# Two graph layers over a dense adjacency matrix: finished block columns taken ahead of their rows, and whole-block transfers

## The chip, the cores and the metric

The kernel runs on one core of a Trainium2 chip. The metric is the device time of one execution in microseconds (us), from the start to the end of the program; lower is better. Three runs of the kernel before took 955.02, 955.76 and 956.75 us (median 955.76). One further execution was profiled; it took 956.43 us, and all rows shown are its rows.

## The reference

With x of 8192 nodes by 64 features and a dense float32 matrix adj of 8192 by 8192, two residual layers are computed:

```
h = relu(layernorm(x));  x = x + adj @ (h * keep / 0.9)      # layer 1, keep = (u >= 0.1)
h = relu(layernorm(x));  x = x + adj @ (h @ W) + b           # layer 2
```

Layer 2 of any node needs the whole of layer 1 for all nodes whose features it sums, so adj (268 MB) is needed twice, and it does not fit on the chip.

## The kernel before

adj is cut into 16 by 16 blocks of 512 by 512 (1 MB each). Block (i, k) joins the 512 nodes of row i to the features of column k. For layer 1, row i needs the blocks (i, 0) to (i, 15). When row i is complete, its new x and then its layer-2 features h2 are computed, and only then may any block of *column* i be used for layer 2. The host lays a block out so that a partition finds its part in one contiguous run; with `PARTS = 2` a block is moved as two half blocks (512 KB each, 4 KB per partition), each into one of `SLOTS = 33` slots of `blocks`.

Work is a list of items (`order_of_items`, L75). A *step* is one 128-row tile of a block multiplied for two 64-row halves of the array at once. Kinds of item:

- `one`: a block for layer 1 alone, even and odd tiles on the two halves (2 steps);
- `both`: block (s, j) below the diagonal, with column j already finished, for layer 1 of row s on one half and layer 2 of row s on the other (4 steps);
- `pair`: two blocks (2p, k) and (2p+1, k) above the diagonal for layer 2, one on each half (4 steps); their layer 1 was done earlier;
- `mix`: layer 2 of a diagonal block beside layer 1 of another block (4 steps).

A block above or on the diagonal has to be on the chip twice, first as `one`, later as `pair` or `mix`. Where it lies near the diagonal (`stays`, L48, with `KEPT = 3`) it is held in its slots in between; the others are read from memory again. Row after row, `order_of_items` takes the items of row s, mixes in the layer-2 items of column s-1 (`late`) at least 10 us after the row began (`ROW_LEAD`, in `merged`, L52), so that h2 of row s-1 is ready, and adds as many of the rereading `pair` items (`again`) as the estimated balance of transfers and matmuls allows; what is left follows after the last row.

`plan` (L111) turns the items into loads, slots and PSUM banks. A slot is taken again by the load that comes next in order, and SP, which issues all loads in order (L275 to L281), first waits until the item that last used the slot is done (`part_used`). `row_sums` has one bank for each parity of the row; `banks` has four for the layer-2 sums (`Sum`); the sums of a `pair` or `mix` item are closed at once, those of the `both` items of a row at the row's end, and VectorE adds each closed sum to `acc` in SBUF (`add_sum`, L412, L419). TensorE waits for `sum_added` before it reuses a bank.

At the end of row s ScalarE copies the row's sums to SBUF (L342), TensorE runs one more item and then transposes them with 8 small matmuls (`turn_row`, L504, L513), and VectorE makes x and h2 of the row (`row_of_layer_1`, L388 to L410), with one square root on ScalarE (L344) and the addition of the bias b (L403). After the last items of each pair of rows, `turn_pair` (L517) multiplies `acc` by W and turns it, VectorE adds it to `rows` (L429, L431), and SP stores.

At the start, SP issues x and u in nine groups (18 transfers, L273 and L274) ahead of the blocks. Per group VectorE, ScalarE and POOL make the layer-1 features (`centre_x` to `drop_x`, L308, L313, L378); POOL's queue also loads W twice and b, spread to all partitions (L300 to L302), and clears `acc` last (L316).

Of the kernel before, what the change touches and what calls it, by code (L numbers as in the profile page):

```python
# [4 lines left out]
P = 128  # L5
N = 8192
# [4 lines left out]
PARTS = 2  # L11
# [14 lines left out]
class Item:  # L26

# [13 lines left out]
class Sum:  # L41


    def __init__(self, p, half, n):
        self.p, self.half, self.first = p, half, n
# [28 lines left out]

def order_of_items():  # L75
    items, waiting = [], []
    for s in range(BLOCKS + 1):
        ones, both, late = [], [], []
        k = s - 1
        if s < BLOCKS:  # L80
            far = [j for j in range(s, BLOCKS) if not stays(s, j)]
            near = [j for j in range(s, BLOCKS) if stays(s, j)]
            ones = [Item("one", [(s, j)], j, s) for j in (near + far if s == 0 else far + near[::-1])]
            both = [Item("both", [(s, j)], j, s) for j in range(s - 1)]
        if s:
            if k % 2 == 0:
                other = ones.pop(0)
                late.append(Item("mix", [(k, k), other.blocks[0]], k, s))
            for p in range(PAIRS - 1, -1, -1):
                if 2 * p + 1 <= k:  # L90
                    t = Item("pair", [(2 * p, k), (2 * p + 1, k)], k)
                    if stays(2 * p, k):
                        late.append(t)
                    else:
                        waiting.append((s + (s < BLOCKS), t))
        again = [t for at, t in waiting if at <= s]
        if s < BLOCKS:
            spare = 2 * STEP * (BLOCKS + s) + 4 * STEP * len(late)
            again = again[:max(0, int((0.97 * spare - BLOCKS * BLOCK_LOAD) / (2 * BLOCK_LOAD - 4 * STEP * 0.97)))]
        waiting = [w for w in waiting if w[1] not in again]  # L100
        if s == BLOCKS:
            items += [t for t in again if t.k < k] + late + [t for t in again if t.k == k]
        else:
            if s:
                late.append(Item("both", [(s, k)], k, s))
            items += merged([both, ones, again, late], ROW_LEAD)
    assert not waiting
    return items


def plan():  # L111
# [42 lines left out]
    for n, t in enumerate(items):  # L154
        if t.kind == "pair":
            t.sum = Sum(t.blocks[0][0] // 2, None, n)
            sums.append(t.sum)
        elif t.kind == "mix":
            t.sum = Sum(t.k // 2, 0, n)
            sums.append(t.sum)  # L160
        elif t.kind == "both":
            if t.row not in row_sum:
                row_sum[t.row] = Sum(t.row // 2, t.row % 2, n)
                sums.append(row_sum[t.row])
            t.sum = row_sum[t.row]
        if t.sum is not None:
            t.sum.last = n
    for index, q in enumerate(sorted(sums, key=lambda q: q.last)):
        q.index = index
# [12 lines left out]
    return items, loads, sums, row_first, row_last, row_end, pair_end, finals  # L182


def bass_gnn(nc, x, adj, u, w, b, out):
# [3 lines left out]
    items, loads, sums, row_first, row_last, row_end, pair_end, finals = plan()  # L189
    closing = {q.last: q for q in sums}  # L190
    final_of = {p: n for n, p in enumerate(finals)}
    final_end = {pair_end[p]: p for p in finals}
    END = len(items)

    with ExitStack() as ctx:  # L195
# [11 lines left out]
        acc = sb("acc", [P, PAIRS, BLK])  # L207
        sums_sb = sb("sums_sb", [P, 2, BLK])
# [24 lines left out]
        x_arrived = [sem(f"x_arrived{n}") for n in range(len(GROUPS))]  # L233
        u_arrived = [sem(f"u_arrived{n}") for n in range(len(GROUPS))]
        weights_arrived = sem("weights_arrived")
        cleared = sem("cleared")
# [13 lines left out]
        row_copied = sem("row_copied")  # L250
        turned_ready = sem("turned_ready")
# [17 lines left out]
        @block.sync  # L269
        def _(sp):  # L270
            for g in range(len(GROUPS)):
                t = group_tiles(g)
                sp.dma_start(rows[:, t, :], x[:, t, :]).then_inc(x_arrived[g], 16)  # L273
                sp.dma_start(u_sb[:, t, :], u[:, t, :]).then_inc(u_arrived[g], 16)  # L274
            for load in loads:  # L275
                before = load["before"]
                if before is not None:
                    sp.wait_ge(part_used, PARTS * before["until"] + before["part"] + 1)
                i, k = load["block"]
                sp.dma_start(blocks[:, load["slot"], :], adj[(i * BLOCKS + k) * PARTS + load["part"], :, :])\  # L280
                    .then_inc(block_arrived[load["slot"]], 16)  # L281
            for n, p in enumerate(finals):
                t = slice(2 * p * TILES, (2 * p + 2) * TILES)
                sp.wait_ge(rows_ready, n + 1)
                sp.wait_ge(turned_taken, BLOCKS + n + 1)
                sp.dma_start(out[:, t, :], rows[:, t, :]).then_inc(stored, 16)
            sp.wait_ge(stored, 16 * PAIRS)

        @block.gpsimd
        def _(pool):  # L290
# [11 lines left out]
            pool.dma_start(bias[:, :], b.rearrange("(a n) -> a n", a=1).to_broadcast([P, D]))\  # L302
                .then_inc(weights_arrived, 16)

            for g, (k0, k1) in enumerate(GROUPS):
                t = group_tiles(g)
                pool.wait_ge(u_arrived[g], 16)
                nc.gpsimd.tensor_scalar(u_sb[:, t, :], u_sb[:, t, :], DROP, 1.0 / (1.0 - DROP),  # L308
                                        ALU.is_ge, ALU.mult).then_inc(keep_ready, 1)
                pool.wait_ge(keep_ready, g + 1)  # L310
                pool.wait_ge(x_scale, g + 1)
                shape = [P, (k1 - k0) * TILES, D]
                nc.gpsimd.tensor_tensor(u_sb[:, t, :], u_sb[:, t, :], square[:, t].unsqueeze(2).to_broadcast(shape),  # L313
                                        ALU.mult).then_inc(keep_scaled, 1)
            pool.wait_ge(xd_ready, len(GROUPS))
            nc.gpsimd.memset(acc[:, :, :], 0.0).then_inc(acc_cleared, 1)  # L316

        @block.scalar
        def _(act):
# [18 lines left out]
            for s in range(BLOCKS):  # L338
                act.wait_ge(part_used, PARTS * (max(row_last[s]) + 1))
                if s >= 2:  # L340
                    act.wait_ge(turned_ready, s - 1)
                nc.scalar.activation(sums_sb[:, s % 2, :], row_sums[:, s % 2, :], ACT.Copy).then_inc(row_copied, 1)  # L342
                act.wait_ge(h2_summed, s + 1)
                nc.scalar.activation(dev2[:, :], square2[:, :], ACT.Sqrt, bias=eps[:, 0:1], scale=1.0 / D)\  # L344
                    .then_inc(h2_dev, 1)

        @block.vector
        def _(dve):
# [7 lines left out]
            def centre_x(g):  # L356
                t = group_tiles(g)
                shape = [P, t.stop - t.start, D]
                dve.wait_ge(x_arrived[g], 16)
# [28 lines left out]
            def row_of_layer_1(s):  # L388
# [23 lines left out]
            def add_sum(q):  # L412
                at = slice(0, P) if q.half is None else slice(q.half * D, (q.half + 1) * D)
                dve.wait_ge(part_used, PARTS * (q.last + 1))
                if q.index == 0:
                    dve.wait_ge(acc_cleared, 1)
                else:
                    dve.wait_ge(sum_added, q.index)
                nc.vector.tensor_tensor(acc[at, q.p, :], acc[at, q.p, :], banks[at, q.bank, :], ALU.add)\  # L419
                    .then_inc(sum_added, 1)  # L420

            def pair_of_rows(p):
# [4 lines left out]
                if n == 0:  # L427
                    dve.wait_ge(biased, BLOCKS)
# [14 lines left out]

            for n in range(END + 2):
                if n in closing:
                    add_sum(closing[n])
                if n - 1 in row_end:
                    row_of_layer_1(row_end[n - 1])
                if n - 1 in final_end:
                    pair_of_rows(final_end[n - 1])  # L450

        @block.tensor
        def _(pe):
# [16 lines left out]

            def layer_2(t, parts, j, half):
# [6 lines left out]
            def multiply(t):  # L478
                s = t.row
                if s is not None and t.n == min(row_first[s]) and s >= 2:  # L480
                    pe.wait_ge(row_copied, s - 1)
                if s == 0:
                    pe.wait_ge(xd_ready, GROUP_OF[t.k] + 1)
                if t.sum is not None:
                    pe.wait_ge(h2_ready, t.k + 1)
                    if t.n == t.sum.first and t.sum.before is not None:
                        pe.wait_ge(sum_added, t.sum.before.index + 1)
# [16 lines left out]
            def turn_row(s):  # L504
# [4 lines left out]
                pe.wait_ge(row_copied, s + 1)  # L509
                for j in range(TILES):  # L510
# [6 lines left out]
            def turn_pair(p):  # L517
                n = final_of[p]
                if n == 0:
                    pe.wait_ge(weights_arrived, 48)  # L520
                pe.wait_ge(turned_taken, BLOCKS + n - 1)
                pe.wait_ge(sum_added, closing[pair_end[p]].index + 1)
# [38 lines left out]
```

## Time and profile before

| | |
|---|---|
| runs | 955.02, 955.76, 956.75 us |
| profiled execution | 956.43 us, of which the span from first to last instruction is 954.6 us |
| TensorE matmuls busy | 914.5 us (96%), 4480 records |
| VectorE, ScalarE, GpSimd busy | 141.7 us, 23.7 us, 33.7 us |
| DMA | 351.00 MB, 95.6% of 16 engines on the block queue |
| blocks moved | 656 half blocks, 344 MB |

A float32 matmul leaves two records in this profile, so a step (two matmuls) is four records. The busy time of TensorE counts a half of the array that works while the other half waits, and the modelled ends of matmuls run into the waits that follow; the time by which the work of TensorE is late has to be taken from the start times. The chain of work that ended last, in order of time, and the tables by stretch show where it waits.

### The profile page before, as it was taken

To read this page: it belongs to the slowest core of one execution; us is meant where nothing else is said; L and a number is where in the kernel's file an instruction comes from. 1 tells how busy PE (TensorE), PEld (TensorE's weight loads), DVE (VectorE), ACT (ScalarE), POOL (GpSimd) and SP (SyncE) were. 2 spreads that over 40 slices of the span, in tenths; PEclk is the share of its full clock that TensorE was granted. 3 is DMA by queue.
4 is the path that set the end of the run, shared out by engine and by line. 5 is a ranking of instruction groups with operands and counts; after the bars stand their busy time and mean duration, and the time that the engine had idled before them with its cause. 6 is when DMAs were issued, how large, how long until landed. Compare 5 with 4: busy or idle time off the path is not lost.

```text
span 954.6 us, 10490 instructions
## 1 busy us (share of the span) xinstructions
PE 914.5 (96%) x4480; PEld 348.6 (37%) x4480; DVE 141.7 (15%) x301; ACT 23.7 (2%) x52; POOL 33.7 (4%) x31
## 2 busy tenths in 40 slices
PE   2888899999999999999999999999999999999998
PEld 0112232333444444443344423443434444443444
DVE  6310101101010101010010100100100200200223
ACT  2100000000000000000000000000000000000000
POOL 7600000000000000000000000000000000000000
PEclk9999999999999999999999999999999999999999
DMA  9999999999999899989999899899899999999992
GB/s 326 410 409 409 409 410 409 409 410 388 410 380 396 297 408 368 381 289 395 361 328 367 291 328 382 333 365 390 315 355 410 364 381 403 368 366 409 409 394 76
DMA packets 98349, 351.00 MB, mean 368 GB/s; under 512 B 10960, under 2 KB 11504, under 8 KB 98304
## 3 DMA queue, kind: packets, MB, share of 16 engines
q1 hardware_dynamic: 98208, 350.27, 95.6%
q8 instruction: 36, 0.59, 0.3%
q0 software_dynamic: 96, 0.07, 0.1%
q14 instruction: 9, 0.07, 0.0%
HBM read 348.19 MB, written 2.10 MB: 367 GB/s over the span
## 4 chain that ended last, share of the span: by engine, by line
PE 83%; DMA 13%; SPq 4%; issue 0%; DVE 0%; DVEq 0%
PE banks L473 45%; PE row_sums L467 37%; DMA blocks<-in_adj 13%; SPq L280 3%; PE turned L526 1%; PE turned L513 1%; SPq L273 0%; SPq L274 0%; DVE rows L429 0%; DVEq L195 0%
## 5 line engine op out<-in xcount | busy, mean ns | idle before, releaser
L467 PE MATMUL row_sums<-blocks,features 128*64 128x512 f32 x2048 | 689.6, 598 | 34.1 <-DMA blocks<-in_adj 31.9
L473 PE MATMUL banks<-blocks,features 128*64 128x512 f32 x2048 | 673.5, 592 | 2.8 <-DMA blocks<-in_adj 2.8
L467 PEld LDWEIGHTS row_sums<-blocks,features 128*64 128x64 f32 x2048 | 213.2, 137 | 327.9 <-issue 238.9
L473 PEld LDWEIGHTS banks<-blocks,features 128*64 128x64 f32 x2048 | 224.9, 137 | 262.4 <-issue 259.6
L419 DVE TENSOR_TENSOR acc<-acc,banks 128x512 f32<-128x512 f32 (+1 forms) x87 | 59.7, 686 | 713.5 <-PE banks L473 640.0
L342 ACT ACTIVATE sums_sb<-row_sums 128x512 f32<-128x512 f32 x16 | 9.6, 597 | 777.7 <-PE banks L473 431.7
L308 POOL TENSOR_SCALAR acc<-acc 128x512 f32<-128x512 f32 (+1 forms) x9 | 18.8, 2092 | 0.8
L393 DVE TENSOR_TENSOR rows<-rows,turned 128x256 f32<-128x256 f32 x16 | 6.7, 421 | 79.8 <-PE turned L513 79.8
L513 PEld LDWEIGHTS turned<-fold,sums_sb 128*64 128x64 f32 x256 | 10.8, 138 | 8.5 <-issue 8.5
L513 PE MATMUL turned<-fold,sums_sb 128*64 128x64 f32 x256 | 10.5, 222 | 0.0
L526 PEld LDWEIGHTS turned<-pair_w,acc 128*64 128x64 f32 x128 | 7.9, 137 | 3.8 <-issue 3.8
L313 POOL TENSOR_TENSOR acc<-acc,square 128x512 f32<-128x512 f32 (+1 forms) x9 | 8.5, 946 | 3.6 <-DVE square L373 3.1
L526 PE MATMUL turned<-pair_w,acc 128*64 128x128 f32 x128 | 8.6, 273 | 0.0
L397 DVE TENSOR_TENSOR centred<-rows,total 128x256 f32<-128x256 f32 x16 | 6.8, 425 | 0.5
L399 DVE TENSOR_TENSOR squares<-centred 128x256 f32<-128x256 f32 x16 | 6.8, 425 | 0.6
L407 DVE SCALAR_TENSOR_TENSOR features<-centred,square 128x256 f32<-128x256 f32 x16 | 6.8, 425 | 0.6
L400 DVE TENSOR_REDUCE square<-squares 128x4 f32<-128x256 f32 x16 | 6.7, 420 | 0.5
L395 DVE TENSOR_REDUCE total<-rows 128x4 f32<-128x256 f32 x16 | 6.7, 420 | 0.5
L344 ACT ACTIVATE dev<-square,eps 128x4 f32<-128x4 f32 x16 | 4.8, 297 | 81.5 <-DVE square L400 81.5
L403 DVE TENSOR_TENSOR rows<-rows,bias 128x256 f32<-128x256 f32 x16 | 6.6, 415 | 0.0
L368 DVE TENSOR_REDUCE square<-features 128x8 f32<-128x512 f32 (+1 forms) x9 | 5.6, 627 | 5.0 <-ACT features L323 5.0
L378 DVE SCALAR_TENSOR_TENSOR features<-features,acc 128x512 f32<-128x512 f32 (+1 forms) x9 | 5.8, 643 | 3.0 <-POOL acc L313 2.8
(25 smaller groups left out, 43.1 us busy)
## 6 DMA issues: line engine op xcount, KB each, us to landing
blocks<-in_adj SPq DMA_DIRECT2D x656, 512.0 KB, 7.8
out<-rows SPq DMA_DIRECT2D x8, 256.0 KB, 2.0
rows<-in_x SPq DMA_DIRECT2D x7, 256.0 KB, 6.8
acc<-in_u SPq DMA_DIRECT2D x7, 256.0 KB, 6.7
rows<-in_x SPq DMA_DIRECT2D x2, 128.0 KB, 2.2
acc<-in_u SPq DMA_DIRECT2D x2, 128.0 KB, 2.5
pair_w<-in_w POOLq DMA_DIRECT2D x2, 16.0 KB, 3.7
bias<-in_b POOLq DMA_DIRECT2D x1, 32.0 KB, 5.5
```

What stands on the lines that cost most here:

```text
L280: sp.dma_start(blocks[:, load["slot"], :], adj[(i * BLOCKS + k) * PARTS + load["part"], :, :])\
L308: nc.gpsimd.tensor_scalar(u_sb[:, t, :], u_sb[:, t, :], DROP, 1.0 / (1.0 - DROP), ALU.is_ge, ALU.mult).then_inc(keep_ready, 1)
L313: nc.gpsimd.tensor_tensor(u_sb[:, t, :], u_sb[:, t, :], square[:, t].unsqueeze(2).to_broadcast(shape), ALU.mult).then_inc(keep_scaled, 1)
L342: nc.scalar.activation(sums_sb[:, s % 2, :], row_sums[:, s % 2, :], ACT.Copy).then_inc(row_copied, 1)
L397: link2(nc.vector.tensor_tensor(centred2[:, :, :], mine, total2[:, :].unsqueeze(2).to_broadcast(shape), ALU.add))
L399: link2(nc.vector.tensor_tensor(squares2[:, :, :], centred2[:, :, :], centred2[:, :, :], ALU.mult))
L407: nc.vector.scalar_tensor_tensor(out=features[:, tiles_of(s), D:2 * D], in0=centred2[:, :, :], scalar=0.0, in1=square2[:, :].unsqueeze(2). ...
L419: nc.vector.tensor_tensor(acc[at, q.p, :], acc[at, q.p, :], banks[at, q.bank, :], ALU.add)\
L467: return nc.tensor.matmul(row_sums[at, s % 2, :], features[:, k * TILES + j, 0:D], tile_of(parts, j), start=first and t.n == row_first[s][ ...
L473: return nc.tensor.matmul(banks[at, t.sum.bank, :], features[:, t.k * TILES + j, D:2 * D], tile_of(parts, j), start=t.n == t.sum.first and ...
L513: done = nc.tensor.matmul(turned[at, s % 2, j * D:(j + 1) * D], sums_sb[:, s % 2, nodes:nodes + D], fold[:, :], start=True, stop=True)
L526: done = nc.tensor.matmul(turned[at, n % 2, j * P:(j + 1) * P], acc[:, p, nodes:nodes + D], pair_w[:, :], start=True, stop=True)
```

## The change

1. `PARTS = 1`, `SLOTS = 15`: a block moves as one transfer of 1 MB (8 KB per partition) into one of 15 whole slots, and its slot is free when its whole item is done. In bytes, 15 whole slots stand where 16.5 stood.
2. `KEPT = 2` instead of 3: fewer blocks are held on the chip between their two uses.
3. `first_rows` orders rows 0 to 3 by a small clock of its own (array and transfer). In it, as soon as h2 of row s-1 is thought to be ready (`H2_LEAD`), column s-1 is taken downwards: beside the items of the rows in progress come items `ahead`, block (i, s-1) for i up to 9, for s = 1, 2, 3, that is 8 + 7 + 6 = 21 blocks. Each is used for layer 1 and layer 2 at once, as `both` is, long before row i is at hand. Its two sums go to the two halves of one of the four `banks`; VectorE adds the layer-2 half to `acc` and the layer-1 half to a new buffer `ahead` in SBUF. At the end of each of the rows 2 to 9 ScalarE copies only one half of `row_sums`, and VectorE adds `ahead` to the other half (`join_ahead`), on which `turn_row` now waits as well (`row_joined`).
4. x and u come in two halves each: 4 transfers of 1 MB instead of 18.
5. b is loaded by POOL's queue after row 7, and added in one instruction for rows 0 to 8 in row 8, then row by row. `ahead` is cleared on POOL after `acc`; the first sum waits for both.
6. The estimate for the `again` items uses 2.49 us per block, and counts the items that are really left in a row.

The diff, cut to its core:

```diff
--- before.py
+++ after.py
...
-PARTS = 2
+PARTS = 1
...
-KEPT = 3
-SLOTS = 33
+KEPT = 2
+SLOTS = 15
+
+AHEAD_ROWS, AHEAD_TO = 3, 10
 SUM_BANKS = 4
 
-STEP, BLOCK_LOAD, ROW_LEAD = 0.858, 2.545, 10.0
+
...
+HALF = N // P // 2
+HALF_OF = [k0 * TILES // HALF for k0, _ in GROUPS]
...
+BIAS_ROW = 8
...
+def layer_2_of(k, ones, waiting):
+    late = []
+    if k % 2 == 0:
+        other = ones.pop(0)
+        late.append(Item("mix", [(k, k), other.blocks[0]], k, k + 1))
+    for p in range(PAIRS - 1, -1, -1):
+        if 2 * p + 1 <= k:
+            t = Item("pair", [(2 * p, k), (2 * p + 1, k)], k)
+            if stays(2 * p, k):
+                late.append(t)
+            else:
+                waiting.append((min(k + 2, BLOCKS), t))
+    if k + 1 < BLOCKS:
+        late.append(Item("both", [(k + 1, k)], k, k + 1))
+    return late
+def layer_1_of(s):
+    far = [j for j in range(s, BLOCKS) if not stays(s, j)]
+    near = [j for j in range(s, BLOCKS) if stays(s, j)]
+    return [Item("one", [(s, j)], j, s) for j in (near + far if s == 0 else far + near[::-1])]
+def first_rows(waiting):
+    items, kept, taken, ready = [], [], set(), []
+    more, here = [], set()
+    array = transfer = 0.0
+    def put(t):
+        nonlocal array, transfer
+        for b in t.blocks:
+            if b in here:
+                here.discard(b)
+            else:
+                transfer += BLOCK_LOAD
+                array = max(array, transfer + LANDING)
+                if t.kind != "pair" and b[1] >= b[0] and stays(*b):
+                    here.add(b)
+        array += t.steps * STEP
+        items.append(t)
+    for s in range(AHEAD_ROWS + 1):
+        ones = layer_1_of(s)
+        own = [Item("both", [(s, j)], j, s) for j in range(s - 1) if (s, j) not in taken]
+        if s:
+            for t in layer_2_of(s - 1, ones, waiting):
+                (kept if all(b in here for b in t.blocks) else more).append(t)
+            more += [Item("ahead", [(i, s - 1)], s - 1, i) for i in range(s + 1, AHEAD_TO)]
+        own += ones
+        while own or any(t.row == s for t in kept + more):
+            kept_now = [t for t in kept if ready[t.k] <= array]
+            more_now = [t for t in more if ready[t.k] <= array]
+            if kept_now and (array < transfer + BLOCK_LOAD + LANDING or not (own or more_now)):
+                t = kept_now[0]
+            elif more_now:
+                t = more_now[0]
+            elif own:
+                t = own[0]
+            else:
+                array = min(ready[t.k] for t in kept + more)
+                continue
+            for queue in (kept, more, own):
+                if t in queue:
+                    queue.remove(t)
+            if t.kind == "ahead":
+                taken.add(t.blocks[0])
+            put(t)
+        ready.append(array + H2_LEAD)
+    return items, kept + [t for t in more if t.kind != "ahead"], taken
 def order_of_items():
+    waiting = []
+    items, left, taken = first_rows(waiting)
+    for s in range(AHEAD_ROWS + 1, BLOCKS + 1):
+        ones = layer_1_of(s)
+        both = left + [Item("both", [(s, j)], j, s) for j in range(s - 1) if s < BLOCKS and (s, j) not in taken]
...
+        if s == BLOCKS:
+            items += [t for t in again if t.k < s - 1] + late + [t for t in again if t.k == s - 1]
+        else:
+            work = STEP * sum(t.steps for t in ones + both + late)
+            loads = BLOCK_LOAD * (len(ones) + len(both) + 1)
+            again = again[:max(0, int((0.97 * work - loads) / (2 * BLOCK_LOAD - 4 * STEP * 0.97)))]
+            items += merged([both, ones, again, late], ROW_LEAD)
...
+        elif t.kind == "ahead":
+            t.sum = Sum(t.row // 2, t.row % 2, n)
+            t.sum.ahead = t.row
+            sums.append(t.sum)
...
-            for g in range(len(GROUPS)):
-                t = group_tiles(g)
-                sp.dma_start(rows[:, t, :], x[:, t, :]).then_inc(x_arrived[g], 16)
-                sp.dma_start(u_sb[:, t, :], u[:, t, :]).then_inc(u_arrived[g], 16)
+            for n in range(2):
+                t = slice(n * HALF, (n + 1) * HALF)
+                sp.dma_start(rows[:, t, :], x[:, t, :]).then_inc(x_arrived[n], 16)
+                sp.dma_start(u_sb[:, t, :], u[:, t, :]).then_inc(u_arrived[n], 16)
...
-            pool.dma_start(bias[:, :], b.rearrange("(a n) -> a n", a=1).to_broadcast([P, D]))\
-                .then_inc(weights_arrived, 16)
...
+            nc.gpsimd.memset(ahead[:, :, :], 0.0).then_inc(acc_cleared, 1)
+
+            pool.wait_ge(part_used, PARTS * (max(row_last[BIAS_ROW - 1]) + 1))
+            pool.dma_start(bias[:, :], b.rearrange("(a n) -> a n", a=1).to_broadcast([P, D]))\
+                .then_inc(bias_arrived, 16)
...
-                nc.scalar.activation(sums_sb[:, s % 2, :], row_sums[:, s % 2, :], ACT.Copy).then_inc(row_copied, 1)
+
+                at = slice(s % 2 * D, s % 2 * D + D) if s in ahead_done else slice(0, P)
+                nc.scalar.activation(sums_sb[at, s % 2, :], row_sums[at, s % 2, :], ACT.Copy).then_inc(row_copied, 1)
...
-                if s == 0:
-                    dve.wait_ge(weights_arrived, 48)
-                nc.vector.tensor_tensor(mine, mine, bias[:, :].unsqueeze(1).to_broadcast(shape), ALU.add)\
-                    .then_inc(biased, 1)
+                if s == BIAS_ROW:
+                    dve.wait_ge(bias_arrived, 16)
+                if s >= BIAS_ROW:
+                    since = rows[:, slice(0 if s == BIAS_ROW else s * TILES, (s + 1) * TILES), :]
+                    nc.vector.tensor_tensor(since, since, bias[:, :].unsqueeze(1).to_broadcast(
+                        [P, since.shape[1], D]), ALU.add).then_inc(biased, 1)
...
+                if q.ahead is not None:
+                    at = slice((1 - q.half) * D, (2 - q.half) * D)
+                    mine = ahead[at, q.p - first_ahead, :]
+                    nc.vector.tensor_tensor(mine, mine, banks[at, q.bank, :], ALU.add).then_inc(sum_added, 1)
+
+            def join_ahead(s):
+                at = slice((1 - s % 2) * D, (2 - s % 2) * D)
+                dve.wait_ge(part_used, PARTS * (max(row_last[s]) + 1))
+                dve.wait_ge(sum_added, ahead_done[s])
+                if s >= 2:
+                    dve.wait_ge(turned_ready, s - 1)
+                nc.vector.tensor_tensor(sums_sb[at, s % 2, :], row_sums[at, s % 2, :],
+                                        ahead[at, s // 2 - first_ahead, :], ALU.add).then_inc(row_joined, 1)
...
+                if n in row_end and row_end[n] in ahead_done:
+                    join_ahead(row_end[n])
...
+            def layer_1_ahead(t, parts, j, half):
+                at = slice(half * D, (half + 1) * D)
+                return nc.tensor.matmul(banks[at, t.sum.bank, :], features[:, t.k * TILES + j, 0:D],
+                                        tile_of(parts, j), start=j == 0, stop=j == TILES - 1)
...
+                    if s - 2 in ahead_done:
+                        pe.wait_ge(row_joined, joined_by[s - 2])
...
+                        elif t.kind == "ahead":
+                            layer_1_ahead(t, t.loads[0], j, 1 - s % 2)
+                            done = layer_2(t, t.loads[0], j, s % 2)
...
+                if s in ahead_done:
+                    pe.wait_ge(row_joined, joined_by[s])
```

## Rows read from the trace of the kernel before

**Rows 1.** The page: busy time, DMA share and granted clock in 40 slices, DMA queues

```profile
PE 914.5 (96%) x4480; PEld 348.6 (37%) x4480; DVE 141.7 (15%) x301; ACT 23.7 (2%) x52; POOL 33.7 (4%) x31
...
PEclk9999999999999999999999999999999999999999
DMA  9999999999999899989999899899899999999992
...
q1 hardware_dynamic: 98208, 350.27, 95.6%
```

**Rows 2.** Stretches: busy PE, PEld, DVE, ACT, POOL; clock, DMA share, GB/s

```profile
25.00:50.00 25.00, 21.41 (x82) 4.21 (x78) 7.29 (x15) 2.06 (x5) 13.85 (x7) 1.00 1.03 409
...
125.00:150.00 25.00, 23.49 (x118) 7.33 (x116) 3.90 (x10) 0.89 (x2) 0.00 (x0) 1.00 1.03 409
...
400.00:425.00 25.00, 25.00 (x133) 10.27 (x130) 1.78 (x3) 0.60 (x1) 0.00 (x0) 1.00 0.86 311
```

**Rows 3.** The chain that ended last, in order of time: start, us, what

```profile
186.27 0.47 PE turned L513 x16
...
273.31 0.47 PE turned L513 x16
...
318.40 0.47 PE turned L513 x16
...
370.37 0.47 PE turned L513 x16
...
427.99 6.23 DMA blocks<-in_adj
...
552.64 7.47 DMA blocks<-in_adj
...
902.49 0.47 PE turned L513 x16
...
924.43 3.43 PE banks L473 x16
```

**Rows 4.** Stretches of the start, same columns as rows 2

```profile
2.00:4.00 2.00, 0.00 (x0) 0.00 (x0) 0.96 (x3) 0.22 (x2) 1.79 (x3) 1.00 0.92 254
4.00:6.00 2.00, 0.00 (x0) 0.00 (x0) 1.38 (x6) 0.71 (x2) 1.12 (x2) 1.00 0.88 194
6.00:8.00 2.00, 0.00 (x0) 0.00 (x0) 1.48 (x5) 0.71 (x2) 1.66 (x2) 1.00 0.84 286
```

**Rows 5.** DMA view of 11 to 15 us, then of 30 to 50 us

```profile
DMA packets 873, 1.61 MB, mean 402 GB/s; under 512 B 99, under 2 KB 99, under 8 KB 873
...
q1 hardware_dynamic: 873, 1.61, 106.1%
...
DMA packets 2251, 8.19 MB, mean 410 GB/s; under 512 B 252, under 2 KB 252, under 8 KB 2250
...
q1 hardware_dynamic: 2250, 8.18, 102.7%
```

**Rows 6.** Instructions of the start in order of time

```profile
6.89 0.42 DVE L378 SCALAR_TENSOR_TENSOR features<-features,acc 128x256 f32<-128x256 f32 x1
...
18.48 9.95 PE L467 MATMUL row_sums<-blocks,features 128*64 128x512 f32 x32 [18.48 <-DMA blocks<-in_adj]
...
28.58 2.42 POOL L308 TENSOR_SCALAR acc<-acc 128x512 f32<-128x512 f32 x1
```

**Rows 7.** Line L280, SP's issues of blocks

```profile
DMA to landing us min/median/max: 3.1/7.8/17.6
```

**Rows 8.** VectorE's instructions by line and shape

```profile
L419 DVE TENSOR_TENSOR acc<-acc,banks 64x512 f32<-64x512 f32 x23 | 15.7, 683 | 238.7 <-PE banks L473 165.2 <-PE row_sums L467 73.6
...
L403 DVE TENSOR_TENSOR rows<-rows,bias 128x256 f32<-128x256 f32 x16 | 6.6, 415 | 0.0
```

**Rows 9.** VectorE at the end of row 10, in order of time

```profile
543.69 0.42 DVE L393 TENSOR_TENSOR rows<-rows,turned 128x256 f32<-128x256 f32 x1 [3.20 <-PE turned L513]
...
546.72 0.42 DVE L407 SCALAR_TENSOR_TENSOR features<-centred,square 128x256 f32<-128x256 f32 x1
```

More of the change, by code:

```diff
@@ L44, in __init__ @@
     def __init__(self, p, half, n):
-        self.p, self.half, self.first = p, half, n
+        self.p, self.half, self.first, self.ahead = p, half, n, None
 def stays(i, k):
@@ L72, in merged @@
     return out
-def order_of_items():
[L76 to L95, printed above, removed]
-        again = [t for at, t in waiting if at <= s]
-        if s < BLOCKS:
-            spare = 2 * STEP * (BLOCKS + s) + 4 * STEP * len(late)
-            again = again[:max(0, int((0.97 * spare - BLOCKS * BLOCK_LOAD) / (2 * BLOCK_LOAD - 4 * STEP * 0.97)))]
-        waiting = [w for w in waiting if w[1] not in again]
[L101 to L106, printed above, removed]
@@ new lines, in order_of_items @@
+def order_of_items():
+    waiting = []
[3 more added lines that the diff above has]
+        both = left + [Item("both", [(s, j)], j, s) for j in range(s - 1) if s < BLOCKS and (s, j) not in taken]
+        left = []
+        late = layer_2_of(s - 1, ones, waiting)
+        again = [t for at, t in waiting if at <= s]
+        if s == BLOCKS:
[5 more added lines that the diff above has]
+            items += merged([both, ones, again, late], ROW_LEAD)
+        waiting = [w for w in waiting if w[1] not in again]
@@ L167, in plan @@
             t.sum.last = n
-    for index, q in enumerate(sorted(sums, key=lambda q: q.last)):
-        q.index = index
+    done, ahead_done = 0, {}
+    for q in sorted(sums, key=lambda q: q.last):
+        q.earlier = done
+        done += 1 if q.ahead is None else 2
+        q.done = done
+        if q.ahead is not None:
+            ahead_done[q.ahead] = done
     bank_free, bank_of = [-1] * SUM_BANKS, [None] * SUM_BANKS
@@ L181, in plan @@
     finals = sorted(range(PAIRS), key=lambda p: pair_end[p])
-    return items, loads, sums, row_first, row_last, row_end, pair_end, finals
+    return items, loads, sums, ahead_done, row_first, row_last, row_end, pair_end, finals
 def bass_gnn(nc, x, adj, u, w, b, out):
@@ L187, in bass_gnn @@
     ALU, ACT, AX = mybir.AluOpType, mybir.ActivationFunctionType, mybir.AxisListType
-    items, loads, sums, row_first, row_last, row_end, pair_end, finals = plan()
+    items, loads, sums, ahead_done, row_first, row_last, row_end, pair_end, finals = plan()
     closing = {q.last: q for q in sums}
@@ L192, in bass_gnn @@
     final_end = {pair_end[p]: p for p in finals}
+    first_ahead = min(ahead_done) // 2
+    joined_by = {s: n + 1 for n, s in enumerate(sorted(ahead_done))}
     END = len(items)
@@ L207, in bass_gnn @@
         acc = sb("acc", [P, PAIRS, BLK])
+        ahead = sb("ahead", [P, max(ahead_done) // 2 - first_ahead + 1, BLK])
         sums_sb = sb("sums_sb", [P, 2, BLK])
@@ L232, in bass_gnn @@
         block_arrived = [sem(f"block_arrived{n}") for n in range(SLOTS)]
-        x_arrived = [sem(f"x_arrived{n}") for n in range(len(GROUPS))]
-        u_arrived = [sem(f"u_arrived{n}") for n in range(len(GROUPS))]
+        x_arrived = [sem(f"x_arrived{n}") for n in range(2)]
+        u_arrived = [sem(f"u_arrived{n}") for n in range(2)]
         weights_arrived = sem("weights_arrived")
+        bias_arrived = sem("bias_arrived")
         cleared = sem("cleared")
@@ L250, in bass_gnn @@
         row_copied = sem("row_copied")
+        row_joined = sem("row_joined")
         turned_ready = sem("turned_ready")
@@ L479, in multiply @@
                 s = t.row
-                if s is not None and t.n == min(row_first[s]) and s >= 2:
+                if s is not None and s >= 2 and t.n == min(row_first[s]):
                     pe.wait_ge(row_copied, s - 1)
+                    if s - 2 in ahead_done:
+                        pe.wait_ge(row_joined, joined_by[s - 2])
                 if s == 0:
@@ L486, in multiply @@
                     if t.n == t.sum.first and t.sum.before is not None:
-                        pe.wait_ge(sum_added, t.sum.before.index + 1)
+                        pe.wait_ge(sum_added, t.sum.before.done)
                 for part in range(PARTS):
@@ L519, in turn_pair @@
                 if n == 0:
[L520 removed]
+                    pe.wait_ge(weights_arrived, 32)
                 pe.wait_ge(turned_taken, BLOCKS + n - 1)
[L522 removed]
+                pe.wait_ge(sum_added, closing[pair_end[p]].done)
                 for j in range(TILES):
```

14 lines of the change are left out of this document (8 added, 6 removed).

## Prediction

> **What bounds the kernel now.** I read the page first [rows 1]: TensorE is busy 96% of the span and the DMA engines 95.6%, so both are candidates, and the question is which one at what time. The stretches [rows 2] answer it: up to about 175 us the DMA engines run without a break at 409 GB/s while TensorE pauses; at 400 us TensorE is full and the DMA share is 0.86. The granted clock stays at 1.00 also where TensorE waits for a third of its time, so pauses cost no clock here.
>
> Busy time hides how late TensorE is (a waiting half counts as busy), so I use the chain [rows 3]. Four steps take 3.43 us there, 0.8575 us each; rows 5 and 6 turn 45.09 us apart with 52 steps between, which leaves 0.50 us for a turned row. I call **offset** the time at which a row turns minus all TensorE work before it. Row 3: 154 steps and 3 turns are 133.6 us, so 186.27 gives 52.7. Row 7: 366 steps and 7 turns are 317.3 us, offset 53.0. Row 15: 976 steps and 15 turns, 844.4 us, offset 58.1. So 53 us are lost before row 4, nothing in rows 4 to 7, and 5.1 us later, in the transfers on the chain at 428 and 553 us. The span is 58.1 + 1024 x 0.8575 (878.1) + 16 x 0.50 (8.0) + 10.4 for the turned pairs and the last store = 954.6 us. The number of steps doesn't change, so the whole effect is in the offset.
>
> **The early offset as a sum.** Where transfers lead, an item starts when the last block it needs has come: offset = X + (blocks loaded so far x T - TensorE work so far), X being when the block stream begins plus landing, T the time of a block. T is 2.56 us at 409.5 GB/s. I followed the planner's loops and took the largest value of the bracket, the **lag**. Before, it is 69 blocks against 141.8 us of work (163 steps, 4 turns): 34.9 us, in row 4. So X = 53.0 - 34.9 = 18.1 us.
>
> **1, 3. Blocks ahead.** Rows 0 to 4 were 80 loads for 200 steps. The change puts into them the 15 blocks of columns 0 to 2 of rows 5 to 9, each 4 steps (3.43 us) for one load: 95 loads for 260 steps when row 4 ends. Its largest lags are at 44 blocks against 91.9 us (106 steps, row 2), 101 against 234.0 us (270 steps, 5 turns, row 5) and 143 against 340.1 us (392 steps, 8 turns, row 8). With the old T these are 20.7, 24.6 and 25.9: blocks ahead alone take 34.9 - 25.9 = 9.0 us away, and the longest wait moves to row 8.
>
> **T of a whole block.** No row of 8 KB exists. Rows of 2 KB and of 4 KB do [rows 5]: 402 and 410 GB/s, so doubling gives 2%, and if that is a fixed cost per packet the next doubling gives 1%: 2.53 us. The queue's occupied time says more: 1.061 x 4 us x 16 engines / 1.61 MB = 42.2 against 1.027 x 20 x 16 / 8.18 = 40.2 engine-us per MB; half of the difference again is 2.5%: 2.50 us. I take 2.52, between the two; the ends are 2.56 (nothing) and 2.49. At 2.52 the lags are 19.0, 20.5 and 20.3, so lag 20.5, 14.4 us less than before (9.0 at 2.56; at 2.49 it is 17.7, 17.2 less). The start of item 147 is nearly as late as that of item 104, so each further 0.01 us of T above this costs 1.4 us.
>
> The Trainium skill, in DMA: Bandwidth & Descriptors, Specifications, gives the fabric a ceiling of 435 GB/s and a core 358 GB/s from HBM. The second is contradicted by 409 in rows 2; by the first a block would take 2.41 us, by an estimate from that page the lag would be 15 us and the total about 930.
>
> **4. Start.** x and u, 4.2 MB, go before the blocks. Between 2 and 8 us they move at 254, 194 and 286 GB/s [rows 4], where 18 small transfers and POOL's three are under way. Four transfers of 1 MB at full rate would save up to 2.9 us of X; if the poor rate belongs to the first microseconds whatever is moved, 0.25 us. I take 1.5. The features come later: the first are ready at 7.3 us before, since 128 KB of x and u suffice [rows 6]; now u's first half comes at about 7 us and they are ready near 10; POOL's groups, 3.6 us each, the eighth at 28.6 and a ninth behind it, slide by some 3 us. The first block is used at about 18 us and the last two of the row land after 50, so this is hidden; the cover is 7 us or more.
>
> **2. Slots.** The late 5.1 us: following the plan, a load normally may start when many transfers are still ahead of it, but at items 162 and 201 to 203 (430 and 550 us) only 1 to 3 *half* blocks lie between the last one the releasing item used and the one that takes its slot, 1.3 to 3.8 us of transfer, and the shortest time from issue to landing is 3.1 us [rows 7]. After the change the least is 4 *whole* blocks (10 us), mostly 7. Comparing every release with every later use, the tightest has 6 us of slack after a 2.1 us landing, where before the slack at the two stalls was 0 and 1.3. That both stalled says that a turnaround costs some 3 us more than that landing, and still 3 of the 6 are left. So I take the 5.0 us away; ends: 0 and 5. The price of `KEPT = 2` is 340 loads instead of 328; in all 340 x 2.52 = 857 us against 886 us of TensorE, so they are covered.
>
> **VectorE.** 21 items ahead give 42 additions of 64 x 512, 8 joins 8 more, at 0.68 us [rows 8]: 34 us on an engine busy 15%. One item ahead costs it 1.4 us per 3.43 us of TensorE, with three banks in turn, so no bank is waited for. Row chain: the join, with an addition ahead of it, takes 1.4 us after the row's end, beside one more item of at least 1.72 us; turning waits for nothing. h2 of a row is ready 3.5 us after the first addition on VectorE [rows 9], about 7 us after the row's end where transfers lead; its first use comes 8.2 us after row 0's end and about as late for rows 1 and 2, over 10 us later on. Margin 1 us, cost nothing; ends 0 and 1 us for each of three rows. **5. Bias**: 8 additions of 0.42 us leave, one of 36 tiles enters in row 8. From 0.42 us for 4 tiles and 0.69 for 8 (by the additions of rows 8) it takes some 2.6 us, and h2 of row 8 is later by 2.2 us; its first use lies 13.7 us of work behind the row's end. Nothing. POOL's wait for it blocks nothing else there; clearing `ahead` ends near 45 us, the first sum comes after 60.
>
> **Sum**, against the profiled execution: 956.43 - 1.5 - 14.4 - 5.0 = 935.5 us. The median of the runs shown lies 0.7 us lower (0.07%), which the range covers.
>
> **Rivals.** (a) *Whole blocks move no faster*: 8 KB go as two packets, T stays 2.56. Then X gains 0.25 to 1.5: 956.4 - 0.9 - 9.0 - 5.0 = 941.5. For it: doubling from 2 to 4 KB gave only 2%. Against: that 2% is a cost per packet. The Trainium skill, same page, SWDGE vs HWDGE vs iDMA, calls 4096 B the preferred largest packet; rows 5 can't show whether one of 8 KB is split. (b) *The order is not what its clock thinks*: h2 or a sum is late, and TensorE waits inside rows 1 to 3, where the lag is near its maximum: three times 1 to 3 us, 938 to 944. (c) *Slower: the slots starve the stream.* With 15 slots, some held, 5 to 6 blocks (13 us) lie between release and landing while transfers lead. If release to landing took longer, by d, every group of 5 loads would lose d, some 26 groups up to row 8: slower than before once d passes 21/26 = 0.8 us, a turnaround of about 14 us. Price with d = 1: 961 us. For it: landings of up to 17.6 us [rows 7]; against: those are transfers queued behind others, and the shortest is 3.1.
>
> **Chances.** Forecast 0.62 (its own range 930 to 940), (a) 0.24, (b) 0.10, (c) 0.04. The range has to reach over (a) with its worst start, 942.2: 930 to 944. A measurement of this kernel can tell 0.2% (1.9 us) from no change. All but (c) are faster by over 1%: faster 0.95, within 0.2% 0.01, slower 0.04.
>
> **What would show it.** Offsets of 35 to 39 us at rows 5 to 15, without a step after row 8; block rate 412 to 419 GB/s up to about 250 us; first block used at 17 to 19 us; no transfer on the chain after row 8; additions twice per item ahead with no wait of TensorE on them. I am wrong if the offset grows in the middle (slots), if the rate stays at 410, or if it is largest in rows 1 to 3 (h2).

## Result and profile after

The kernel after takes 932.1 us (four runs, 932.02 to 932.63); the runs of the kernel before beside it have a median of 956.25 us. The ratio is 0.9746, 95% interval 0.9725 to 0.9766: 2.5% faster. The profiled execution took 932.63 us with a span of 930.8 us, against 956.43 and 954.6 before. One execution of a run further down, the profiled one of slots13, ran at a granted clock of 0.85 throughout and took 1075.03 us; it stands outside every comparison.

The page of the kernel after, parts 1 to 3 (compare [rows 1]):

```profile
PE 900.5 (97%) x4480; PEld 356.8 (38%) x4480; DVE 175.6 (19%) x343; ACT 23.8 (3%) x52; POOL 35.6 (4%) x32
...
DMA  9999999999999999999999999899999999999993
GB/s 370 421 421 421 421 421 421 421 421 420 421 422 421 421 421 420 421 418 404 395 391 359 347 381 395 324 374 352 362 346 376 366 415 400 370 358 421 386 423 155
...
q1 hardware_dynamic: 50688, 362.83, 96.8%
```

The core moves 12.6 MB more (362.83 against 350.27), in half the packets, at 421 GB/s instead of 409 wherever transfers lead. VectorE works 34 us longer, as its 50 new additions should, and it holds nobody up: the table of waits has no wait of TensorE on a sum or a join, and the chain below has no piece of VectorE before the last addition.

The chain that ended last, in order of time (compare [rows 3]):

```profile
9.68 27.36 DMA blocks<-in_adj
...
39.15 25.70 DMA blocks<-in_adj
...
104.72 20.12 DMA blocks<-in_adj
...
228.56 0.47 PE turned L630 x16
...
248.33 19.35 DMA blocks<-in_adj
...
292.07 0.46 PE turned L630 x16
...
875.25 0.47 PE turned L630 x16
```

The last transfer on the chain ends at 268 us, in row 5; the two of 428 and 553 us are gone. The offsets: row 3 turns after 226 steps and 3 turns (195.3 us), offset 33.3; row 5 after 298 steps and 5 turns (258.0), 34.1; row 15 after 972 steps and 15 turns (841.0), 34.3. Before they were 52.7, 53.0 and 58.1. The rest of the span, 896.5 us of work and tail, is what it was, so the whole gain of the span is the fall of the final offset by 23.8 us.

The start in stretches, columns as in [rows 4]:

```profile
2.00:4.00 2.00, 0.00 (x0) 0.00 (x0) 0.00 (x0) 0.22 (x2) 1.23 (x2) 1.00 0.88 217
4.00:6.00 2.00, 0.00 (x0) 0.00 (x0) 0.00 (x0) 0.00 (x0) 0.00 (x0) 1.00 0.94 393
6.00:8.00 2.00, 0.00 (x0) 0.00 (x0) 1.03 (x4) 0.42 (x1) 0.00 (x0) 1.00 0.98 409
8.00:10.00 2.00, 0.00 (x0) 0.00 (x0) 1.53 (x6) 0.72 (x2) 0.90 (x1) 1.00 1.02 427
```

From 4 us on x and u move at full rate, and VectorE begins 3.4 us later than before (6.35 against 2.97 us). Nobody waits for it: the first features are ready at 11.5 us and the first block is used at 16.60. The least cover in row 0 is 3.4 us: the features for blocks 2 and 3 are ready at 18.8 us, and block 2 is used at 22.2. The table of waits does put 5.3 us of TensorE's weight loads in row 0 down to features, but the features they need had been ready for 4 us and more.

### The profile page after: what moved, and what is told of

The parts are those of the page before. It is cut to its first block, busy times and chain, and to the rows that moved or that the text cites. A ratio compares the mean times of both kernels' runs of the same rounds, so it can differ in the third digit from the quotient of the medians.

```text
span 930.8 us, 10203 instructions
## 1 busy us (share of the span) xinstructions
PE 900.5 (97%) x4480; PEld 356.8 (38%) x4480; DVE 175.6 (19%) x343; ACT 23.8 (3%) x52; POOL 35.6 (4%) x32
## 3 DMA queue, kind: packets, MB, share of 16 engines
q1 hardware_dynamic: 50688, 362.83, 96.8%
## 4 chain that ended last, share of the span: by engine, by line
PE 89%; DMA 10%; SPq 1%; issue 0%; DVE 0%; DVEq 0%
PE banks L583 47%; PE row_sums L572 36%; DMA blocks<-in_adj 10%; PE banks L578 4%; PE turned L643 1%; SPq L363 1%; PE turned L630 1%; SPq L357 0%; SPq L356 0%; DVE rows L532 0%; DVEq L274 0%
## 5 line engine op out<-in xcount | busy, mean ns | idle before, releaser
L583 PE MATMUL banks<-blocks,features 128*64 128x512 f32 x2048 | 670.0, 592 | 1.2 <-DMA blocks<-in_adj 1.2
L572 PE MATMUL row_sums<-blocks,features 128*64 128x512 f32 x1880 | 604.9, 596 | 25.9 <-DMA blocks<-in_adj 25.7
L583 PEld LDWEIGHTS banks<-blocks,features 128*64 128x64 f32 x2048 | 226.6, 137 | 261.9 <-issue 261.9
L572 PEld LDWEIGHTS row_sums<-blocks,features 128*64 128x64 f32 x1880 | 197.7, 138 | 272.2 <-issue 260.8
L509 DVE TENSOR_TENSOR acc<-acc,banks 128x512 f32<-128x512 f32 (+1 forms) x108 | 74.2, 687 | 625.9 <-PE banks L583 568.5
L578 PE MATMUL banks<-blocks,features 128*64 128x512 f32 x168 | 72.5, 592 | 0.0
L578 PEld LDWEIGHTS banks<-blocks,features 128*64 128x64 f32 x168 | 23.0, 137 | 24.2 <-issue 24.2
L430 ACT ACTIVATE sums_sb<-row_sums 128x512 f32<-128x512 f32 (+1 forms) x16 | 9.5, 595 | 749.8 <-PE row_sums L572 375.1
L514 DVE TENSOR_TENSOR ahead<-ahead,banks 64x512 f32<-64x512 f32 x21 | 14.4, 685 | 0.7
L522 DVE TENSOR_TENSOR sums_sb<-row_sums,ahead 64x512 f32<-64x512 f32 x8 | 5.5, 688 | 34.3 <-PE row_sums L572 34.3
```

What stands on the lines that cost most here:

```text
L430: nc.scalar.activation(sums_sb[at, s % 2, :], row_sums[at, s % 2, :], ACT.Copy).then_inc(row_copied, 1)
L514: nc.vector.tensor_tensor(mine, mine, banks[at, q.bank, :], ALU.add).then_inc(sum_added, 1)
L572: return nc.tensor.matmul(row_sums[at, s % 2, :], features[:, k * TILES + j, 0:D], tile_of(parts, j), start=first and t.n == row_first[s][ ...
L578: return nc.tensor.matmul(banks[at, t.sum.bank, :], features[:, t.k * TILES + j, 0:D], tile_of(parts, j), start=j == 0, stop=j == TILES - 1)
L583: return nc.tensor.matmul(banks[at, t.sum.bank, :], features[:, t.k * TILES + j, D:2 * D], tile_of(parts, j), start=t.n == t.sum.first and ...
```

## Experiments

Every kernel was timed beside the kernel before on one chip, whose median was 955.3 to 956.0 us in the different sets. In all kernels for which a final offset is given here row 15 turns after the same 972 steps, so its time less 841.0 us is the final offset.

### Halves again

```diff
-PARTS = 1
+PARTS = 2
-SLOTS = 15
+SLOTS = 30
```

> The kernel after, but blocks again as two half transfers of 512 KB (4 KB per partition) into 30 half slots, the same bytes and the same order of items. Theory A (the block rate sets the early offset, and it rose from 409 to 421 GB/s because the rows grew to 8 KB): the rate falls back to 409 to 410 GB/s, a block takes 2.56 us, the lag rises from 17.7 to 24.2 us (half blocks arrive half a block earlier, hence not 25.9), the offset of rows 8 to 15 from 34.1 to 40.7, time 938.8 us, with the longest wait in row 8. Rival B (the rate rose for another reason, or the finer grain makes up for it): rate 421, offset 33 to 34, time 931 to 932.

939.55 us (939.35 to 939.71). The page's rates, and the last row's turn in the chain:

```profile
GB/s 370 409 409 409 408 409 409 409 409 410 409 408 409 409 409 409 407 409 409 408 409 408 364 400 381 319 381 363 346 357 366 372 391 409 391 355 407 408 409 136
```

```profile
365.32 16.93 DMA blocks<-in_adj
...
881.99 0.47 PE turned L630 x16
```

The rate is back at 409, the last transfer on the chain ends at 382 us, in row 8, where the lag of 143 blocks was expected, and the final offset is 41.0 against 40.7. Theory A holds, with a time 0.75 us above the expected 938.8. The whole block is worth 7.5 us in this kernel.

### Fewer and more blocks ahead

```diff
-AHEAD_ROWS, AHEAD_TO = 3, 10
+AHEAD_ROWS, AHEAD_TO = 3, 8     # to8;  3, 12 in to12
```

> The kernel after with columns 0 to 2 taken ahead down to row 7 instead of row 9 (AHEAD_TO = 8, 15 blocks ahead instead of 21). Theory A (offset = X + largest of loads x T minus work): the lag rises from 17.7 to 23.1 us, its place moves to item 98 in row 4 or after, offset 39.5, time 937.5. Rival B (the early offset is set by row 0, where no column is finished yet, and blocks ahead beyond a few bring nothing): 932.

936.98 us (936.7 to 937.15), so 4.9 of the 5.4 us.

> The kernel after with columns 0 to 2 taken ahead down to row 11 (AHEAD_TO = 12, 27 blocks ahead). Theory A: the lag falls from 17.7 to 16.7 us, the value at item 19 that no block ahead can lower, since nothing of column 0 is finished before; the slots get tighter (2.3 us to spare after the bare landing instead of 6.2), which the 3 us of a real turnaround may turn into a stall of up to 1 us: 931.1 us, up to 932. Rival B (row 1 to 3 waits on h2 or sums grow with the number of items ahead): 933 or more.

931.0 us (930.59 to 931.43). The chain of to12:

```profile
38.92 25.85 DMA blocks<-in_adj
...
310.96 0.47 PE turned L630 x16
...
873.54 0.47 PE turned L630 x16
```

Its last transfer ends at 65 us, before any item ahead, and the final offset is 32.5. By the plan the early loss is now the part that blocks ahead can't lower: 16 blocks of row 0 at two steps each and the few until h2 of row 0 is ready. Both times follow the sum X + lag within 0.6 us, and neither rival B holds.

### The transfers part and KEPT on the kernel before

```diff
-PARTS = 2
+PARTS = 1
-KEPT = 3
-SLOTS = 33
+KEPT = 2
+SLOTS = 16
```

> The kernel before with the transfers part alone: whole blocks of 1 MB into 16 slots, KEPT = 2; old order of rows, no blocks ahead, x, u and bias as before. Theory A: block rate 421 GB/s, lag 31.4 instead of 34.9 us, and the stalls at 430 and 550 us gone since 4 or more whole blocks lie between release and use: 956.2 - 3.5 - 5.0 = 947.7 us. Rival B (the late stalls came from the order of items, not from the slots): 952.7. Rival C (whole blocks bring little without the blocks ahead): 955.

947.97 us (947.86 to 948.55; ratio 0.9927, interval 0.9912 to 0.9941), against 947.7.

> The kernel before with KEPT = 2 alone (33 half slots, half transfers, 340 blocks loaded instead of 328). Theory A (late stalls are slots that come free too late): the early offset stays at 53, the late stalls shrink from 5 us to 0 to 2 us (tightest now at items 128 to 130): 951 to 953 us. Rival B (the order or the balance of reloads made them): 956 or more, since 12 more blocks are loaded.

951.72 us (951.15 to 952.48; ratio 0.9964, interval 0.9951 to 0.9976). Rows 5 and 15 of b_kept2, from its chain:

```profile
269.39 0.47 PE turned L513 x16
...
893.78 0.47 PE turned L513 x16
```

Row 5 (250 steps, 5 turns, 216.9 us) has an offset of 52.5 us and row 15 of 52.8: the early loss of the kernel before without the 5 us that followed. `KEPT = 2` also changes the order of the items, so this run alone doesn't part late slots from order. The trace of the kernel before does. In the 4 us before the transfer of 428 us the stream had room:

```profile
424.00:428.00 4.00, 4.00 (x36) 1.87 (x33) 3.21 (x9) 0.30 (x1) 0.00 (x0) 1.00 0.75 266
```

It moved 266 GB/s where 409 was possible, and the transfer was issued at 427.99, as a step of TensorE ended: SP was waiting for a slot. By the plan the least number of half blocks between a release and the load that takes the slot is 1 before and 11 in b_kept2. So the late stalls were slots that came free too late, and holding fewer blocks cures them although 12 more are loaded. In b_whole row 15 turns at 890.55, offset 49.6: from there to 52.8 is what the faster stream is worth in the old order.

### Fewer slots

```diff
-SLOTS = 15
+SLOTS = 12     # slots12;  13 in slots13
```

> The kernel after with 12 slots instead of 15. By the plan the tightest release has its landing 1.2 us too late after a 2.1 us landing latency (with 15 slots: 6.2 us to spare). Theory A (a turnaround costs some 5 us beyond the transfer itself, read from the stalls of the kernel before, where slack 0 and 1.3 stalled and 3.1 did not): one or more stalls of 4 us, time 936 to 941. Rival B (turnaround is the bare 2.1 us): 932 to 934. Rival C (the stream itself starves while transfers lead, d per group of slots): block rate below 421 GB/s before 250 us, time above 945.

962.35 us, 955.56 to 967.67 in nine runs; ratio 1.0062, interval 1.0032 to 1.0091: slower than the kernel before. The page and the chain of slots12:

```profile
GB/s 376 421 421 421 421 422 418 393 410 387 422 398 402 397 393 397 393 360 377 361 367 352 323 389 373 297 365 356 348 315 346 349 389 410 364 367 408 394 423 274
```

```profile
262.14 0.47 PE turned L630 x16
...
374.18 0.46 PE turned L630 x16
...
471.61 0.47 PE turned L630 x16
...
671.95 0.47 PE turned L630 x16
...
900.03 0.47 PE turned L630 x16
```

Both marks of rival C are there: the stream is full for seven slices of 24 us and then gives way, long before 250 us, and the time is above 945. Its mechanism, a stream that starves while transfers lead, is the small part. Row 3 turns at 228.14 us, no later than in the kernel after; row 4 (262 steps, 4 turns, 226.7 us) has an offset of 35.4, row 5 is 3 us later than in the kernel after, and over 20 of the 25 us by which the final offset (59.0) is larger come behind it, in nearly every row. This looks like theory A's stall many times over. Theory A had priced the tightest release alone; in the plan stalls follow each other, because an item that waits also frees its slots later.

> The kernel after with 13 slots. With 12 the kernel took 962, thirty us more, since stall follows stall from row 4 to row 14: each stalled item also holds back the release of the next slots. If I let every load wait for its slot, and every item for its loads, through the whole plan, then 962 wants an overhead of 3.7 us from a release to the landing beside the 2.49 us of transfer. Theory A (one such overhead, 3.5 to 4 us, for all releases): with 13 slots the offset ends at 34.5 to 35, 932.5 to 933.5 us. Rival B (the stream starves as soon as fewer whole slots are free, at any overhead): half of the loss of 12 slots or more, 945.

934.57, 935.82 and 937.39 us in its three timed executions, and no row of its profile is used. The loss is 2.5 to 5.3 us, more than theory A's and far from rival B's. If the plan is worked through with every load waiting for its slot, an estimate, 12 slots want 3.6 to 4.3 us between a release and the landing beside the transfer to give the measured times, and 13 slots 4.5 to 5: no single constant fits both, and what the difference is stays open. What is shown: 15 slots lose 0.2 us behind row 5, 13 lose some us, 12 lose 30. The times with 12 slots scatter by 12 us (by 0.6 us after); the two slowest executions, 967.6 and 967.7 us, also have the lowest granted clocks, 0.993 and 0.995, so not all of the scatter need be slots.

### The start

In groups18, x and u come in nine groups again (18 transfers); the rest is as after.

```diff
-            for n in range(2):
-                t = slice(n * HALF, (n + 1) * HALF)
+            for g in range(len(GROUPS)):
+                t = group_tiles(g)
```

> The kernel after with x and u again in nine groups, 18 transfers, ahead of the blocks; all else as after. Theory A: the start of the stream is later by the 1.5 us that the offset X fell (18.1 to 16.6): 933.6 us, and the first 6 us move less than 300 GB/s again. Rival B (the late bias, not the large transfers, cleared the start): 932.1, no change.

934.46 us (934.08 to 934.9). Its stretch from 4 to 6 us moves 226 GB/s and the first block is used at 18.71 us, 2.1 us later. Theory A holds, and the cost is 2.4 us where 1.5 was expected.

In bias_early, the bias is loaded behind W at the start, `BIAS_ROW = 0`, and no wait on POOL.

> The kernel after with the bias loaded at the start on POOL's queue and added row by row from row 0, as before the change. Theory A (large transfers of x and u cleared the start): 932.1 to 932.4, since 32 KB are 0.1 us of the stream. Rival B (128 rows of 256 B written by the software queue disturb the first transfers): 1 us or more, 933.1.

934.11 us (933.9 to 934.67). The DMA view of 8 to 10 us in bias_early:

```profile
DMA packets 51, 0.30 MB, mean 150 GB/s; under 512 B 10, under 2 KB 10, under 8 KB 16
...
q1 hardware_dynamic: 36, 0.29, 39.7%
q0 software_dynamic: 15, 0.01, 37.1%
```

The same stretch in the kernel after:

```profile
DMA packets 127, 0.85 MB, mean 427 GB/s; under 512 B 22, under 2 KB 23, under 8 KB 23
...
q1 hardware_dynamic: 116, 0.85, 101.6%
q0 software_dynamic: 11, 0.00, 0.4%
```

Fifteen packets of POOL's queue hold the engines for 37% of 2 us on 16 engines, 12 engine-us, and the stream drops to 150 GB/s. Nine of them are of 4 bytes; the six that carry the bias, 2 KB each, take nearly all of it, about 2 us each. Rival B holds: the bias at the start costs 2.0 us.

The run changes the load and the row-by-row addition together. The first block is already used 1.3 us later (17.90 against 16.60 us) and row 5 turns 1.6 us later, so most of the loss is there before the bias is added to any row. The load is not slow by itself either. In the kernel after, behind row 7, the same 32 KB pass in the stretch from 370 to 372 us:

```profile
DMA packets 139, 0.80 MB, mean 401 GB/s; under 512 B 29, under 2 KB 29, under 8 KB 45
...
q0 software_dynamic: 32, 0.03, 4.8%
```

There all of its packets together take 1.5 engine-us beside a full stream, which loses some 20 GB/s for 2 us. Why the same packets take 2 us each at 8 us and under 0.1 us at 370 no run here shows.

> The kernel after with the whole old start: x and u in 18 transfers, bias loaded early and added row by row. Alone, the 18 transfers cost 2.4 us and the early bias 2.0. Theory A (both spoil the same first 10 us, so they overlap; the old start is what made X 18.1 instead of 16.4): 934 to 935. Rival B (they add up): 936.5.

934.82 us (934.33 to 935.37): both together cost 2.7 us, not 4.4. They spoil the same microseconds; either alone takes most of the loss.

> The kernel after with the two small loads of W moved behind row 7 too, beside the bias; W is first used after row 15. Theory A (small rows of POOL's queue slow the first transfers): the stretch from 2 to 4 us, 217 GB/s after, comes near 400, and the start is earlier by up to 0.9 us: 931.2 to 931.7. Rival B (the poor rate at 2 to 4 us is the first transfers' own): 932.1.

932.04 us (931.82 to 932.38), the 932.1 of the kernel after within the scatter; the stretch from 2 to 4 us moves 242 instead of 217 GB/s. Rival B: W costs 0.1 us by the medians, less than the scatter, and the poor stretch from 2 to 4 us is mostly the transfers' own.

> The kernel after with columns taken ahead down to row 11 (AHEAD_TO = 12) and W loaded late. Theory A (both act on the early offset, one on the lag, one on X, so they add up): 931.0 less what w_late brings, 930.1 to 930.7. Rival B (no gain from W): 931.0.

930.49 us (930.17 to 930.99; ratio 0.9741, interval 0.9728 to 0.9755), the fastest of all kernels here, 1.6 us below the kernel after. to12 alone had 931.0, so 1.1 us of it are the six more blocks ahead. The other 0.5 lies inside theory A's range, but w_late alone brought 0.1 and one kernel's runs differ by up to 0.8, so that W adds to it isn't shown.

## Why the prediction was right

Predicted 935.5 us, measured 932.63 in the profiled execution and 932.1 in the median. The mechanism held, and the miss is one mis-sized term, T.

- **The frame** (offset = X + lag, nothing else changes) held: 896.5 us of work and tail in both.
- **X**: forecast 16.6, found 34.1 - 17.7 = 16.4, as what is left of the offset. The 1.5 us were put down to larger transfers; the runs show 2.4 us for these alone, 2.0 for the late bias alone and 2.7 for both. So the late bias, which I priced at nothing at the start, is nearly an equal cause, and that X came out within 0.2 us is partly luck. The 2.9 us that I gave as the most don't follow from the three stretches alone: at 409 GB/s what they moved takes 3.6 of 6 us, which saves 2.4. The sum leaves 0.8 us open here: with the same old start X is 49.6 - 31.4 = 18.2 in b_whole, and 19.0 in start_old, whose row 15 turns at 877.71.
- **T** was the mis-sized term: taken as 2.52 us, found 2.49 (1.0486 MB at 421 GB/s). At 2.49 the lag is 17.7 instead of 20.5, and the sum becomes 932.7, the measurement within 0.1. The rule I used, that a second doubling of the packet brings half of the first, gave 1% by the rates and 2.5% by the occupied time; measured are 2.9% (409 to 421). The occupied time was the better witness, and the middle between it and the rates the wrong choice. Rival (a), no faster, falls with the 421 GB/s and with the run on halves, where the old rate costs 7.5 us. Its mechanism falls too: the kernel after moves its blocks in half the packets, so a row of 8 KB goes as one and not as two.
- **Late stalls**: 5.0 us taken away, and b_kept2 shows 5 us less at row 15. I had named the slots as a whole; the part that does it is `KEPT = 2`.
- **Blocks ahead** at old T were to bring 9.0 us. In the runs, b_whole to start_old (order and blocks ahead, same T, same start) is 947.97 - 934.82 = 13.2 us, where the lags at 2.49, 31.4 and 17.7, give 13.7 (b_whole has 16 slots, start_old 15).
- **VectorE, h2, bias in row 8**: no cost, as forecast. The one long addition took 2.55 us against 2.6 estimated. The cover of the later features, which I gave as 7 us or more, was 3.4 at the least; that too was enough.
- **Rival (c)**, starved slots, does not happen at 15. In the run with 12 the missing slots do cost 30 us, but mostly behind row 5, where it had priced the groups up to row 8 while transfers lead. Its price, and my slack by single releases, were too simple: they find where the loss begins and not what it costs.
- **Rival (b)**: row 3 turns at offset 33.3, below row 5's 34.1, and the chain has no piece of VectorE or ScalarE in rows 1 to 3, so these rows hold no wait beside the transfers that counts.

Three of the signs named beforehand were missed on the fast side: offsets of 34.1 to 34.3 where 35 to 39 were named, 421 GB/s instead of 412 to 419, and the first block used at 16.60 us instead of 17 to 19. The first two are the mis-sized T; the third is the start, which with whole blocks brings 2.8 us up to the first block (19.41 in start_old). That no transfer is on the chain after row 8, and no wait of TensorE on an addition, came as said.

The parts don't add up the same way in every order. From the kernel before: `KEPT = 2` 4.3 us, whole blocks another 3.8, order and blocks ahead 13.2, start 2.7, together 23.9. But taking whole blocks away from the kernel after costs 7.5. At the old rate the longest lag there has 143 blocks behind it, and each pays the slower rate; in the old order the longest lag has 58 to 69. Blocks ahead make a faster stream worth more.

## What to carry to other kernels

Where transfers lead at first and the array later, measure how late the array is at fixed points of its work and write that as the start of the stream plus the largest of loads x T minus work; work that uses a block twice should go before that maximum, and this brings nothing more once the maximum lies before the first such work. Count, for each buffer, the transfers between its release and its next use: that number has to cover the turnaround everywhere, and holding less on the chip can be worth more than the rereading it costs. Look at what small transfers of another queue do to the stream where the stream is the bound, even if they are a ten-thousandth of its bytes: the same load cost 2.0 us at the start and next to nothing at 370 us.

## What the runs showed of the hardware

- One core's stream from memory ran at 409 GB/s with rows of 4 KB and at 421 with rows of 8 KB, same bytes per slot and same order. The Trainium skill (DMA: Bandwidth & Descriptors, Specifications) gives 358 GB/s from HBM for a core, half of what a stack gives to two, which both rates exceed with one core at work, and a ceiling of 435 for the fabric, which they stay under.
- 32 KB spread from 256 B to 128 partitions by POOL's queue at the start took the stream down to 150 GB/s for 2 us and cost 2.0 us (bias_early), where its bytes are 0.1 us; the six packets that began from 8 to 10 us took about 2 us each. The same load at 370 us took 1.5 engine-us in all beside a stream of 401 GB/s (after). The two loads of W at the start, 16 KB each, cost 0.1 us or nothing (w_late).
